# Four transformer layers on one core: reordered loads and stores in the first attention, unit keys' parts moved into its loop, and constant matmuls at each attention's begin

## The chip, the cores and the metric

The kernel is one program on one of the eight cores of a Trainium2 chip. The metric is the device time of one execution in microseconds. A core has five engines with instruction streams of their own: TensorE (PE, matrix products), VectorE (DVE), ScalarE (ACT), GpSimd (POOL) and SyncE (SP, which here only issues transfers). They meet through semaphores. Each engine works strictly through its own list, so an instruction that waits holds back all that stands behind it, transfers that the engine issues included.

## The reference

`x` has 16 batches of 64 tokens with 256 features; `ctx` has the same shape. Four layers follow each other, each of them an attention and a feed-forward:

```python
x = x + L0_xattn(layernorm(x), ctx, ctx)      # 8 heads of 8 features x 256 positions, softmax
x = x + L0_ffn(layernorm(x))                  # ternary weights, quantized activations, two gelus
x = x + L1_xattn(layernorm(x), ctx, ctx)      # as L0, q and k of each head scaled to unit length, x 5
x = x + L1_ffn(layernorm(x))                  # mixture of 8 experts, top 2
x = x + gamma * L2_xattn(layernorm(x), ctx, ctx)   # as L0
x = x + L2_ffn(layernorm(x))                  # mixture of 32 experts, top 8
x = x + L3_xattn(layernorm(x), ctx, mask)     # 16 heads, quantized projections
x = x + L3_ffn(layernorm(x))                  # mixture of 16 experts, top 4
```

In layers 0 to 2 attention takes the 64 x 256 block of one batch as 8 heads of 8 rows: for each head a 256 x 256 matrix of scores, each of them a sum over only 8 features. Scores are wanted at float32 accuracy.

## The kernel before, in words

**Stages.** One function, `attention` (from L417), builds the attentions of layers 0, 1 and 2; `ternary_feed_forward` (from L1614) builds the feed-forward of layer 0; a generic mixture the others. Each is one or more blocks, and at a block's end all engines meet.

**Parts.** A float32 value is split into three bfloat16 values, high, middle and low (`Parts`, L203 on: `high` and `mid` on ScalarE, `take_high` and `take_mid` on GpSimd or VectorE). The parts of normed `x` are stored to DRAM in `q_parts` (`store_q`, L507), those of `ctx` in `k_plain` (`store_k`, L516), and loaded again per batch in another arrangement: `load_q` (L528) writes 288 KB, `load_k` (L538) three times 96 KB. The 72 rows of a head (9 pairs of parts times 8 features) then give a float32 score in one bfloat16 matmul. Tokens are worked in five groups, `CUTS = ((0, 1), (1, 2), (2, 4), (4, 6), (6, 8))`, of tiles of 128 tokens, which are two batches each.

**The loop of an attention with maxima (layers 0 and 2).** For each batch and head TensorE first computes scores into `p_max` (`max_scores`, L669; three buffers), VectorE takes the row maxima (L925), GpSimd splits the 128 x 16 maxima of a batch into three parts (`split_max`, L1019), TensorE turns them (`turn_maxima`, L682), ScalarE copies them (L785) and issues their transfer into rows 72 to 74 of `q` (L790). TensorE then computes the scores again, transposed and with the maximum subtracted (`scores`, L697), ScalarE exponentiates (`exps`, L792), TensorE weighs the values (`weigh`, L715, f32 matmuls), ScalarE copies the result (`copy_out`, L800). Maxima run two batches ahead of the rest (`AHEAD = 16` heads, before the loop). Within a step the order on TensorE is written out by hand, with m for a head's maxima, digits for score pairs, w to z for quarters of the weighing of the batch before, and t for a turn:

```python
FIRST_ORDER = "0mm1mmtmm2mm3mmt"
STEP_ORDER = "mm0mm1wxmmyz2mm3t"
PLAIN_ORDER = "0w1x2yz3"
```

The results go to DRAM (`store_out`, L560) and come back by tile (`load_whole`, L565); VectorE inverts the softmax sums in quarters of a tile between maxima (`invert`, L929, from head n = 61 on, one tile each 16 heads), and GpSimd divides and adds to `x` (`add_tile`, L1034, at even b from 8 on). Layer 1 has no maxima: its queries are normed by `HeadNorm` (L253 on: sums over heads by TensorE, `total_first` and `total_others`; root on ScalarE; inverse on VectorE; spread back by TensorE, `spread_out`).

**SyncE's order in layer 0.** After the first loads: `store_k(0)`, `store_q(0)`, `load_k(0)`, `load_q(0)`, `load_q(1)`, `load_k(1)`, `store_k(1)`, `store_q(1)`, `load_k(2)`, `load_q(2)`, `load_q(3)`, `load_k(3)`, `store_k(2)`, `store_q(2)`. Then, for each step b: `load_k(b + 4)`, `load_q(b + 4)`, `store_out(b - 1)` (which waits for ScalarE's copy of batch b - 1, made in step b), for b = 0 and 1 `store_k(b + 3)` and `store_q(b + 3)`, and from b = 3 on `load_whole(b - 3)`. There are eight slots for `q` and `k`, so a load of batch b + 8 waits until batch b has been scored. ScalarE issues the values' four transfers of 1 MB (`load_v`: one before the loop, the others at the ends of steps 1, 5 and 9).

**Unit keys.** Layer 1's keys are worked out ahead (`UnitKeys`, L318 on). `ctx` in another arrangement (1 MB, `load`) is loaded at the end of step 1; GpSimd adds squares (`add_square`, two feature tiles in each of steps 4 to 7); VectorE clamps the sums behind head 84 (`clamp`). In the feed-forward of layer 0 ScalarE takes the root (`root`, L365), VectorE the reciprocal (`invert`, L369), and GpSimd makes for each of 8 feature tiles the five instructions of `split` (scale, high, rest, middle, low), while SyncE stores each part as it is made (`store_unit_keys`, 24 transfers of 64 KB).

**The feed-forward of layer 0, first block.** VectorE norms `x`, takes row maxima, waits for the mean of the weights (TensorE, from ScalarE's sums over the two raw weights), rounds the first weight in three passes over 128 x 2048 (L1584 to L1586), works out the scale in a dozen short instructions, then rounds each of 8 tiles of `x` in three passes of 128 x 256; TensorE turns a tile (L1707), VectorE copies it (L1785), TensorE multiplies (L1714), ScalarE applies gelu, squares, gelu again. Behind the eighth copy VectorE rounds the second weight and takes maxima of the eight results.

## Time and profile before

| | us |
|---|---|
| median of three runs (1333.0 to 1335.53) | 1334.82 |
| the profiled execution's own time | 1329.65 |
| its span, first to last instruction | 1327.8 |

| stretch of the span | us | TensorE busy | granted clock, mean |
|---|---|---|---|
| attention of layer 0 | 0 to 169.8 | 120.93 | 0.92 |
| feed-forward of layer 0 | 169.8 to 254 | 31.70 | 0.59 |
| attention of layer 1 | 254 to 352 | 79.29 | 0.91 |
| feed-forward of layer 1 | 352 to 501.5 | 130.58 | 0.91 |
| attention of layer 2 | 501.5 to 642 | 111.10 | 0.84 |
| all behind it | 642 to 1327.8 | 612.37 | 0.94 |

TensorE is the busiest engine over the span (82%), before VectorE (51%), ScalarE (48%) and GpSimd (40%). The granted clock is the share of TensorE's full 2.4 GHz that was granted; 0.50 is 1.2 GHz. Two cautions on it: it shows 1.00 before the first change that is on record (71 us), though the matmuls there run at the lower level, so their durations tell the clock better; and a busy share says nothing on whether TensorE was working at 1.2 or at 2.4 GHz.

### The profile page before, as it was taken

Reading aid. Unit: us, or ns where it says so; the run is one execution under the profiler, and the core shown is the slowest. Engines: PE = TensorE matmul, PEld = TensorE weight load, DVE = VectorE, ACT = ScalarE, POOL = GpSimd, SP = SyncE. Lnnn points to the kernel's source line nnn. Section 1 sums busy time; section 2 is a strip of 40 time slices with the busy share of each in tenths; the row PEclk is TensorE's granted clock in tenths of the full one; section 3 lists DMA queues with packets and bytes.
Section 4 is the critical chain, followed back from the end, with each engine's and each line's share of the span. In section 5 each row is a group of like instructions: output and inputs, shape, how many; then the busy total and the mean of one; then the engine's idle time right before and its main releaser. Section 6 shows DMA issues by size and latency. Waiting matters only on the chain. (4 is left out here: it accounts for less than half of the span.)

```text
span 1327.8 us, 19221 instructions
## 1 busy us (share of the span) xinstructions
PE 1086.0 (82%) x6655; PEld 778.3 (59%) x6656; DVE 672.9 (51%) x1377; ACT 636.7 (48%) x1007; POOL 535.4 (40%) x592
## 2 busy tenths in 40 slices
PE   2988714489599994999489999999867569999997
PEld 0445401344288871555378888888634357888886
DVE  5667588741453336787643333333568653333333
ACT  4556537579544434677333344444374334344332
POOL 5132243001236652122256666666310316666663
PEclk9989855789879995899689999999988778999999
DMA  5655121168314314342133343333000013333331
GB/s 172 206 153 161 51 83 28 40 144 224 99 57 123 111 43 132 105 135 77 50 99 111 111 164 121 114 118 114 21 8 1 2 56 125 114 118 114 112 115 55
DMA packets 65796, 132.42 MB, mean 100 GB/s; under 512 B 9291, under 2 KB 33035, under 8 KB 65094
## 3 DMA queue, kind: packets, MB, share of 16 engines
q1 hardware_dynamic: 62326, 124.15, 31.5%
q10 hardware_dynamic: 3408, 7.47, 1.7%
q8 instruction: 35, 0.57, 0.2%
q14 instruction: 27, 0.22, 0.1%
HBM read 115.55 MB, written 15.45 MB: 99 GB/s over the span
## 5 line engine op out<-in xcount | busy, mean ns | idle before, releaser
L1404 POOL TENSOR_TENSOR f_hid<-f_gated,f_coef 128x512 f32<-128x512 f32 x152 | 224.0, 1475 | 161.6 <-DVE f_gated L1435 150.2
L1435 DVE TENSOR_TENSOR f_gated<-f_act_g,f_p_u 128x512 f32<-128x512 f32 x152 | 104.5, 688 | 261.9 <-PE f_p_u L1267 258.1
L796 ACT ACTIVATE a_probs<-a_p_sc 128x1024 f32<-128x1024 f32 x192 | 189.1, 1020 | 31.7 <-PE a_p_sc L710 24.1
L1344 ACT ACTIVATE f_hid_hi<-f_hid 128x512 fp32r<-128x512 f32 x152 | 96.1, 632 | 206.4 <-POOL f_hid L1404 206.3
L925 DVE TENSOR_REDUCE a_maxes<-a_p_max 128x2 f32<-128x512 f32 x256 | 160.0, 680 | 55.0 <-PE a_p_max L677 54.7
L1439 DVE TENSOR_TENSOR f_hid_lo<-f_hid,f_hid_hi 128x512 fp32r<-128x512 f32 x152 | 105.6, 695 | 151.3 <-ACT f_hid_hi L1344 150.9
L1339 ACT ACTIVATE f_act_g<-f_p_g 128x512 f32<-128x512 f32 x152 | 90.8, 597 | 160.8 <-PE f_p_g L1267 160.7
L677 PE MATMUL a_p_max<-a_k,a_q 72*128 72x256 bf16 x512 | 98.9, 318 | 50.4 <-DMA a_q<-q_parts 40.4
L710 PE MATMUL a_p_sc<-a_q,a_k 75*128 75x256 bf16 (+1 forms) x768 | 121.0, 287 | 10.5 <-ACT a_probs L796 4.7
L1280 PE MATMUL f_p_y<-f_hid_hi,f_down_hi 128*128 128x512 f32 x304 | 119.5, 393 | 7.0 <-issue 7.0
L1391 POOL TENSOR_TENSOR f_up_lo<-f_w,f_up_hi 128x512 fp32r<-128x512 f32 x76 | 98.0, 1290 | 56.7 <-ACT f_up_hi L1329 56.7
L1280 PE MATMUL f_p_y<-f_hid_lo,f_down_hi 128*128 128x512 f32 x304 | 119.0, 392 | 0.0
L1280 PE MATMUL f_p_y<-f_hid_hi,f_down_lo 128*128 128x512 f32 x304 | 119.0, 391 | 0.0
L730 PE MATMUL a_p_out<-a_probs,all_v 128*32 128x256 f32 x1536 | 111.8, 406 | 1.2 <-ACT a_probs L796 1.2
L710 PEld LDWEIGHTS a_p_sc<-a_q,a_k 75*128 75x128 bf16 (+1 forms) x768 | 70.4, 102 | 58.9 <-issue 22.8
L1391 POOL TENSOR_TENSOR f_down_lo<-f_w,f_down_hi 128x256 fp32r<-128x256 f32 x76 | 70.7, 931 | 76.6 <-ACT f_down_hi L1334 76.6
L677 PEld LDWEIGHTS a_p_max<-a_k,a_q 72*128 72x128 bf16 x512 | 47.0, 108 | 90.3 <-issue 52.1
L1267 PE MATMUL f_p_g<-f_x_hi,f_up_hi 128*128 128x512 f32 x304 | 96.0, 398 | 0.0
L1267 PE MATMUL f_p_g<-f_x_hi,f_up_lo 128*128 128x512 f32 x304 | 95.4, 395 | 0.0
L1267 PE MATMUL f_p_g<-f_x_lo,f_up_hi 128*128 128x512 f32 x304 | 95.4, 395 | 0.0
L1267 PE MATMUL f_p_u<-f_x_hi,f_up_hi 128*128 128x512 f32 x304 | 95.3, 395 | 0.0
L1267 PE MATMUL f_p_u<-f_x_lo,f_up_hi 128*128 128x512 f32 x304 | 94.7, 393 | 0.0
(283 smaller groups left out, 1682.8 us busy)
## 6 DMA issues: line engine op xcount, KB each, us to landing
f_w<-in_w SPq DMA_DIRECT2D x76, 384.0 KB, 3.5
f_coef<-coef SPq DMA_DIRECT2D x51, 512.0 KB, 3.7
a_q<-q_parts SPq DMA_DIRECT2D x48, 288.0 KB
a_k<-k_plain SPq DMA_DIRECT2D x96, 96.0 KB
outs<-a_out SPq DMA_DIRECT2D x48, 128.0 KB, 1.7
a_whole<-outs SPq DMA_DIRECT2D x48, 128.0 KB, 2.6
q_parts<-a_q_part SPq DMA_DIRECT2D x48, 96.0 KB, 3.2
a_k<-k_unit SPq DMA_DIRECT2D x24, 192.0 KB
```

Of the source, the lines that this page charges most:

```text
L677: last = nc.tensor.matmul(p_max[:, n % 3, t * D:(t + 1) * D], q_of(b, h, ROWS)[:, t * P:(t + 1) * P], k_of(b, h, ROWS), start=True, stop=True)
L710: last = nc.tensor.matmul(p_sc[pair % 2][:, h % 2, t * D:(t + 1) * D], k_of(b, h, K_ROWS)[:, t * P:(t + 1) * P], q_of(b, h, K_ROWS), start ...
L730: last = nc.tensor.matmul(p_out[32 * j:32 * j + 32, 0:D], m.v[:, b, at:at + 32], probs[b % 2][:, h, t, :], start=(quarter == 0), stop=(qua ...
L796: nc.scalar.activation(probs[b % 2][:, 2 * pair:2 * pair + 2, :, :].rearrange("p h t d -> p h (t d)"), p_sc[pair % 2][:], ACT.Exp, scale=s ...
L925: nc.vector.tensor_reduce(maxes[b % 3][:, :, h], p_max[:, n % 3, :].rearrange("p (t d) -> p t d", t=NK), axis=AX.X, op=ALU.max, negate=Tru ...
L1267: last = nc.tensor.matmul(p[:], w_[n][:, (2 * k + s) * P:(2 * k + s + 1) * P], x_[:, k, tok], start=(i == 0), stop=(i == len(passes) - 1))
L1280: last = nc.tensor.matmul(p_y[o][c][:], w_[n][:, o * P:(o + 1) * P], h_[n][c][:], start=start and i == 0, stop=stop and i == len(passes) - ...
L1344: nc.scalar.activation(hid_hi[slot(t, 2)][c][:], hid[c][:], ACT.Copy).then_inc(hid_hi_done, 1)
L1391: nc.gpsimd.tensor_tensor(lo[slot(t, 2)][:], w[slot(t, 2)][:, cols], hi[slot(t, 2)][:], ALU.subtract).then_inc(lo_ready, 1)
L1404: nc.gpsimd.tensor_tensor(hid[c][:], gated[c][:], coef[slot(t, 2)][:, c * 512:(c + 1) * 512], ALU.mult).then_inc(hid_done, 1)
L1435: nc.vector.tensor_tensor(gated[c][:], act_g[c][:], p_u[c][:], ALU.mult).then_inc(gated_done, 1)
L1439: nc.vector.tensor_tensor(hid_lo[slot(t, 2)][c][:], hid[c][:], hid_hi[slot(t, 2)][c][:], ALU.subtract).then_inc(hid_lo_done, 1)
```

## The change

SyncE's order in layer 0 puts all stores of parts, and the loads of batches 0 to 7, before the loop; layer 2 likewise. In the loop the loads are now those of batch b + 7, from b = 1 on, and stand between `store_out(b - 1)` and `load_whole(b - 3)`. At the very begin ScalarE waits for the first tile of `ctx` before it issues the large loads. The unit keys are loaded in the prologue, behind the first values. Their squares are added in steps 2 to 5, the clamp is behind head 68, the root at the end of step 6, the inverse behind head 76, and the five-part splits are one feature tile in each of steps 8 to 15, all of it in the attention's loop; the feed-forward only stores them, with no waits. TensorE gets a filler, 128 x 128 by 128 x 256 bfloat16 matmuls of a constant tile into a part of `p_out` that nothing reads before it is written again: in layer 0, 44 of them once the first query parts are ready, in layer 2, 64; in both, two more behind each of the first ten heads of maxima; in layer 1, 20 ahead of `total_others` and 16 behind it.

```diff
@@ SyncE, layer 0, before the loop
                     store_k(1)
+                    store_k(2)
+                    load_k(2)
                     store_q(1, 0)
                     store_q(1, 1)
-                    load_k(2)
+                    load_k(3)
                     load_q(2)
                     load_q(3)
-                    load_k(3)
-                    store_k(2)
+                    store_k(3)
                     store_q(2, 0)
                     store_q(2, 1)
+                    load_k(4)
+                    store_k(4)
+                    load_q(4)
+                    store_q(3, 0)
+                    store_q(3, 1)
+                    load_k(5)
...
@@ SyncE, loop
-                    elif b + 4 < B:
-                        load_k(b + 4)
-                        load_q(b + 4)
                     if b >= 1:
                         store_out(b - 1)
-                    if with_max and b in (0, 1):
-                        if layer == 0:
-                            store_k(b + 3)
-                        store_q(b + 3, 0)
-                        store_q(b + 3, 1)
+                    if with_max and b >= 1 and b + 7 < B:
+                        load_k(b + 7)
+                        load_q(b + 7)
                     if b >= 3:
                         load_whole(b - 3)
@@ TensorE
+                def keep_busy(count):
+
+                    for _ in range(count):
+                        nc.tensor.matmul(p_out[:, 0:D], m.filler[:, 0:P], m.filler[:], start=True, stop=True)
+
+                pe.wait_ge(m.filler_set, 1)
...
                     pe.wait_ge(masks_loaded[1], 16)
+                    keep_busy(20)
                     unit.total_others(pe)
+                    keep_busy(16)
...
                 if with_max:
+                    parts.ready(pe, 2, 0)
+                    keep_busy(44 if layer == 0 else 64)
                     for n in range(AHEAD):
                         max_scores(n)
+                        if n < HEADS + 2:
+                            keep_busy(2)
@@ ScalarE, layer 0, begin
+                    act.wait_ge(keys_loaded[0], 16)
                     act.dma_start(m.x[:, 1:NI, :], a["x"][:, 1:NI, :]).then_inc(m.x_loaded[1], 16)
+                    key_parts.high(0)
                     act.dma_start(keys[:, 1:NI, :], a["ctx"][:, 1:NI, :]).then_inc(keys_loaded[1], 16)
-                    act.wait_ge(keys_loaded[0], 16)
-                    key_parts.high(0)
...
                     load_v(0)
+                    unit_keys.load(act, a)
@@ ScalarE, loop
-                        if layer == 0 and b == 1:
-                            unit_keys.load(act, a)
+                        if layer == 0 and b == 6:
+                            unit_keys.root(act)
@@ VectorE, loop over heads
-                            if n == 10 * HEADS + 4:
+                            if n == 8 * HEADS + 4:
                                 unit_keys.clamp(dve)
+                            if n == 9 * HEADS + 4:
+                                unit_keys.invert(dve)
@@ GpSimd, loop
-                        if layer == 0 and 4 <= b < 8:
-                            for c in range(2 * (b - 4), 2 * (b - 3)):
+                        if layer == 0 and 2 <= b < 6:
+                            for c in range(2 * (b - 2), 2 * (b - 1)):
                                 unit_keys.add_square(pool, c)
+                        if layer == 0 and b >= B - CH:
+                            if b == B - CH:
+                                for g, (lo, hi) in enumerate(CUTS):
+                                    pool.wait_ge(k_stored[g], 16 * (hi - lo))
+                            for what in range(5):
+                                unit_keys.split(pool, one, what, b - (B - CH))
```

## Rows read from the trace of the kernel before

**Rows 1.** Timeline, ScalarE, attention of layer 0: copies of finished batches (start, duration, what)

```profile
54.66 0.39 ACT L804 ACTIVATE a_out<-a_p_out 128x256 f32<-128x256 f32 x1 [3.71 <-PE a_p_out L730]
...
66.97 0.38 ACT L804 ACTIVATE a_out<-a_p_out 128x256 f32<-128x256 f32 x1 [1.35 <-PE a_p_out L730]
...
82.13 0.39 ACT L804 ACTIVATE a_out<-a_p_out 128x256 f32<-128x256 f32 x1 [3.55 <-PE a_p_out L730]
...
123.27 0.38 ACT L804 ACTIVATE a_out<-a_p_out 128x256 f32<-128x256 f32 x1 [1.27 <-PE a_p_out L730]
...
129.79 0.38 ACT L804 ACTIVATE a_out<-a_p_out 128x256 f32<-128x256 f32 x1 [1.55 <-PE a_p_out L730]
...
141.17 0.38 ACT L804 ACTIVATE a_out<-a_p_out 128x256 f32<-128x256 f32 x1 [2.66 <-PE a_p_out L730]
...
161.86 0.39 ACT L804 ACTIVATE a_out<-a_p_out 128x256 f32<-128x256 f32 x1 [1.19 <-PE a_p_out L730]
```

**Rows 2.** Timeline, ScalarE, attention of layer 2: first and last such copy

```profile
543.32 0.38 ACT L804 ACTIVATE a_out<-a_p_out 128x256 f32<-128x256 f32 x1 [3.17 <-PE a_p_out L730]
...
634.32 0.38 ACT L804 ACTIVATE a_out<-a_p_out 128x256 f32<-128x256 f32 x1 [1.19 <-PE a_p_out L730]
```

**Rows 3.** Timeline, 58 to 72 us: the unit keys' load, and TensorE's longest wait

```profile
58.04 0.70 ACTq L340 DMA_DIRECT2D early_ukeys<-in_ctx_heads  x1
...
71.81 1.01 PE L677 MATMUL a_p_max<-a_k,a_q 72*128 72x256 bf16 x4 [4.36 <-issue]
```

**Rows 4.** Timeline, VectorE and TensorE, 106 to 131 us: three waits

```profile
106.11 0.81 DVE L361 TENSOR_SCALAR early_ulength<-early_ulength 128x256 f32<-128x256 f32 x1 [0.32 <-POOL early_ulength L357]
...
110.35 0.28 PE L692 MATMUL a_p_out<-all_ident_bf,a_neg 128*24 128x128 bf16 x2 [0.87 <-POOL a_neg L1032]
...
130.60 0.55 DVE L935 RECIPROCAL a_inv<-a_whole 128x64 f32<-128x64 f32 x1 [2.52 <-DMA a_whole<-outs]
```

**Rows 5.** Timeline, first steps of the attentions of layers 0 and 2: TensorE, and query parts

```profile
37.20 1.03 PE L710 MATMUL a_p_sc<-a_q,a_k 75*128 75x256 bf16 x4 [2.81 <-DMA a_q<-a_neg_t]
...
49.83 1.94 PE L730 MATMUL a_p_out<-a_probs,all_v 128*32 128x256 f32 x16
...
54.52 0.61 PE L710 MATMUL a_p_sc<-a_q,a_k 75*128 75x256 bf16 x4
...
504.78 0.42 DVE L241 TENSOR_TENSOR a_q_part<-all_xn,a_q_part 128x256 bf16<-128x256 f32 x1 [0.48 <-ACT a_q_part L229]
...
515.55 6.16 PE L677 MATMUL a_p_max<-a_k,a_q 72*128 72x256 bf16 x22 [18.07 <-DMA a_q<-q_parts]
...
526.46 1.03 PE L710 MATMUL a_p_sc<-a_q,a_k 75*128 75x256 bf16 x4 [1.25 <-DMA a_q<-a_neg_t]
```

**Rows 6.** Timeline, feed-forward of layer 0: VectorE, and TensorE's first transposition

```profile
179.81 1.75 DVE L369 RECIPROCAL early_uinverse<-early_ulength 128x256 f32<-128x256 f32 x1
...
181.82 1.70 DVE L1584 TENSOR_SCALAR b_tmp<-b_raw,b_sums 128x2048 f32<-128x2048 f32 x1
...
193.82 0.39 PE L1707 MATMUL b_p_t<-all_ident_bf,b_xq 128*128 128x128 bf16 x2 [14.00 <-DVE b_xq L1586]
...
214.25 1.28 DVE L1584 TENSOR_SCALAR b_tmp<-b_raw,b_sums 128x2048 f32<-128x2048 f32 x1
```

**Rows 7.** Timeline, GpSimd: two unit-key tiles' begins; a maximum's split and the tile behind it

```profile
187.85 0.72 POOL L377 TENSOR_TENSOR early_ukeys<-early_ukeys,early_uinverse 128x256 f32<-128x256 f32 x1
...
191.45 0.72 POOL L377 TENSOR_TENSOR early_ukeys<-early_ukeys,early_uinverse 128x256 f32<-128x256 f32 x1
...
132.37 0.22 POOL L1026 TENSOR_TENSOR a_neg<-a_maxes,a_one 128x16 bf16<-128x16 f32 x1 [7.88 <-DVE a_maxes L925]
...
133.44 0.72 POOL L1039 TENSOR_TENSOR a_prod<-a_whole,a_inv 128x256 f32<-128x256 f32 x1
```

**Rows 8.** Timeline, ScalarE at the begin: a change of activation table

```profile
8.22 1.28 ACT L136 ACT_TABLE_LOAD   x1
```

**Rows 9.** Timeline, TensorE, attention of layer 1: the sums over heads

```profile
266.44 4.77 PE L284 MATMUL a_p_max<-a_qn_square,a_gather 128*128 128x256 f32 x14 [7.73 <-DVE a_qn_square L272]
```

35 lines of the change are left out of this document (23 added, 12 removed).

## The prediction, written before the result was known

> **What bounds the kernel now.** The page says that TensorE is busiest. The question for this change is how much of that it spends waiting or at 1.2 GHz, and where. So the stretches come first (front table): the attentions of layers 0 and 2 have the same loop of 16 batches, yet one takes 169.8 us and the other 140.5. Then I time both loops by ScalarE's copies of finished batches, the last thing done for a batch on the way out. In layer 0 the first copy is at 54.66 and the last at 161.86: 107.2 us [rows 1]. In layer 2 they are at 543.32 and 634.32: 91.0 us for the same 15 intervals, 6.07 on average [rows 2]. The reader is to see two long intervals in layer 0: 66.97 to 82.13 (15.16) and 129.79 to 141.17 (11.38), where a loaded one, 123.27 to 129.79, takes 6.52 [rows 1].
>
> The timelines give their causes. The unit keys' 1 MB is issued at 58.04, with values just ahead of it, and TensorE then stands 4.36 us before it gets the next keys and queries for maxima at 71.81 [rows 3]. At 130.60 VectorE has waited 2.52 us for a tile of outputs to come back, with heads of maxima queued behind it [rows 4]. And at 110.35 TensorE has waited 0.87 us for GpSimd, after VectorE's clamp at 106.11 waited for squares that GpSimd was still adding [rows 4]. Behind each wait TensorE also runs at 1.2 GHz for a while: four score matmuls take 1.01 us at 71.81 [rows 3], 0.61 at 54.52 [rows 5]. So a wait of 1 to 4 us costs 2 to 9.
>
> The second place is each attention's begin: in layer 0 the first scores are at 37.20, at 1.03 for four, and the faster level is first seen at 54.52; in layer 2, from 526.46 to the first copy at 543.32, it is the same [rows 2, 5]. The third is the feed-forward of layer 0, where VectorE holds the path: the unit keys' reciprocal of 1.75 us stands in its list, and a pass over 128 x 2048 takes 1.70 us while GpSimd splits keys and 1.28 when it has stopped [rows 6].
>
> **Layer 0, loads and stores ahead.** Queries of batch 6 are now issued before the loop ends its first step, and nothing of 2 MB can push in front: the keys' load is 30 us earlier, and only the values are left at step 1. The wait at 71.81 goes. Loads for batch b + 7 are five steps ahead of their use. From step 9 on no load is left, so the outputs that VectorE wanted at 130.60 come back without a queue before them. Against that, in steps 4 to 8 `load_whole` now stands behind four load issues. It has about one step before VectorE's first quarter; I take no wait, at most one such as at 130.60, 5.3 us with its slow stretch (11.38 - 6.07). What is late next is TensorE's own chain, as in layer 2. So the loop falls from 107.2 to layer 2's 91.0: -16.2.
>
> **Layer 0's head.** ScalarE gets its first tile of `ctx` sooner, and the chain of group 0 with it. But the unit keys' 1 MB now lands in the prologue, on the same issuing queue ahead of the transfer that the first scores wait for (2.81 us before 37.20 [rows 5]), and SyncE stores group 1's queries later than now. Below, the wait of 2.81 goes; above, 1 MB more, bounded by TensorE's longest wait behind the same load, 4.36 [rows 3]. I take 0 for the first scores. From there to the first copy it was 17.46 us (54.66 - 37.20), in layer 2 16.86 (543.32 - 526.46) [rows 1, 2, 5]: -0.6.
>
> **Unit keys in the loop.** Added to 91.0: VectorE's clamp, 0.81 and perhaps its wait of 0.32 [rows 4]; the reciprocal, 1.75 [rows 6]; ScalarE's root between exponentials, which takes two table changes of 1.28 [rows 8]. At nothing if slack hides them (a step without inverses is shorter than 6.52, so there is some), at most their sum, 5.4, plus one slow stretch of 5.3 = 10.7. They stand on different engines in steps 6 and 7 and each has part of a step's slack. I take +4. GpSimd's splits: a tile takes 3.60 us (187.85 to 191.45), a maximum's split 1.07 (132.37 to 133.44), and every second step adds an `add_tile`, two instructions of 0.72 with their gaps, about 1.5 [rows 7]. That is 6.2 in a step of 6.52 [rows 1]: it fits by 0.3, so 0, up to what the third rival says. The last two splits are behind the last maxima; behind them come `add_tile(4)` and `(5)`, which VectorE's last inverses need: 2 x 3.6 + 3 x 1.5 and one more split, 15 us, beside two steps and a tail that last some 20. Nothing.
>
> **The feed-forward of layer 0.** The reciprocal goes from VectorE's list: -1.75, less perhaps 0.2 as the mean of the weights is then waited for; I take -1.6 [rows 6]. From the first pass at 181.82 to TensorE's first transposition at 193.82 VectorE works beside GpSimd for 12.0 us. At the ratio of the two passes, 1.28 / 1.70, that becomes 9.0: -3.0. The short instructions there hold waits too, so 1.0 (three passes at 0.42 less, 1.3, rounded down) is the least. The loop of eight tiles behind it was in part paced by the same passes; TensorE and ScalarE hold it near, so -0.9 of at most 3. Sum -5.5, range -2.6 to -8. SyncE's 24 stores now come at once behind the two raw weights in one queue. They cost nothing unless they share with the second weight; then up to 3.
>
> **Layer 1.** 14 f32 matmuls in 4.77 us begin at the lower level [rows 9]. At the upper they would be at most halved, -2.4, but they wait for squares; the 16 fillers behind them fill a wait. -1, between 0 and -2.4.
>
> **Fillers in layers 0 and 2.** No row has this matmul; the nearest are four of 256 columns in 1.03 or in 0.61, so 0.26 or 0.15 each [rows 5]. The 64 take 9.8 to 16.5 us and have from 505.20 (504.78 + 0.42) to 515.55, 10.35 [rows 5]. All slow they would delay the start by 6; the clock should rise on the way: 0, with up to +3 for a late rise. They can gain only if the faster level lasts until the first scores. The maxima of the lead are paced by VectorE and gain nothing. Behind the tenth head the fillers end, and there are a turn, five heads and the wait of 1.25 us before 526.46 [rows 5]; in layer 0 the wait is 2.81. A wait of 0.87 was followed by a slow stretch [rows 4]. Moreover, in layer 0 TensorE multiplied scores almost without a break from 37.20 to 49.83 and stayed slow; it got fast only some 4.7 us after the f32 weighing had begun [rows 5]. So I expect the level to be lost before step 0 and steps 0 and 1 to be as now: 0.
> The Trainium skill (TensorE: Matmul & The Clock Gate, "The HAM clock gate") says that any sustained matmul activity releases the throttle, and that long idle gaps bring it back. By that rule the fillers work and layer 2 gains what rival 1 gives; 12 us of score matmuls that released nothing speak against it.
>
> **Sum.** -16.2 - 0.6 + 4 - 5.5 - 1 + 0 = -19.3. The profiled execution took 1329.65, so 1310.35. The median of the runs lies 5.17 higher (1334.82); the same distance kept, 1315.5.
>
> **Rivals.**
> 1. The fillers hold the faster level into steps 0 and 1. The 16.86 us before layer 2's first copy become a short first step and two thirds of a second, 1.67 x 6.07 = 10.1: -6.8; in layer 0 the same if the start isn't late. 1315.5 - 13.6 = 1302, with layer 2 alone 1309. For it: 64 matmuls without a gap just ahead of the loop. Against it: what stands above.
> 2. The moved work costs what it can: 10.7 instead of 4 in steps 6 and 7, and one wait for returned outputs, 5.3: 1315.5 + 12 = 1327.5. For it: the clamp's wait of today comes back in step 6 with the same distance to the squares. Against it: each has slack.
> 3. Slower: GpSimd becomes the bound in steps 8 to 13. If its instructions in the loop are over 5% longer than beside a busy VectorE in the feed-forward (0.3 of 6.2), each turn of the maxima waits for `split_max`; from about 0.9 us on, 18%, each wait is followed by a slow stretch, 5.3 a step. Six steps: +32, 1347. Against it: VectorE's reduction reads PSUM there, and GpSimd's first instruction of a split is 0.72 in the feed-forward, as `add_tile`'s is in the loop [rows 7].
> 4. The prologue's order starves the first scores by a backlog longer than 4.4 us: with 8 us, 1323.
>
> **How the numbers follow.** Forecast 0.57 (own range 1309 to 1322), rival 1 0.18, rival 2 0.13, rival 4 0.07, rival 3 0.05. I call 0.2%, 2.7 us, the least that can be told here. All but rival 3 are faster by more: 0.93; 0.03 in between, 0.04 slower. The range takes in the upper half of rival 1 and most of rival 2: 1300 to 1327.
>
> **What would show it.** In the trace after: no TensorE wait over 2 us in the loop of layer 0, and first to last copy in 92 to 99 us. A wait before the score matmuls of step 7, with table changes on ScalarE. GpSimd nearly without a pause in steps 8 to 13, and TensorE's turn there not over 0.9 us late. VectorE's 128 x 2048 pass at 1.28 in the feed-forward and the first transposition some 5 us after its begin sooner than 24.0 (193.82 - 169.8). Score matmuls of step 0 in both layers at 1.03 for four; 0.61 there proves rival 1. I am wrong in the main point if the interval with the 15.16 stays above 9, or if steps 8 to 13 average above 7.5.

## The result, and the profile after

The changed kernel takes 1345.46 us (median of five runs, 1341.03 to 1350.37) against 1333.19 for the kernel before (five runs): ratio 1.0083, 95% interval 1.0053 to 1.0113. I had forecast 1315.5 and gave slower a chance of 0.04. The profiled execution took 1350.37, its span is 1348.6 us, 20.8 longer than before.

The page of the kernel after; compared with before, TensorE is busy longer and there is more of it at a lower clock:

```profile
span 1348.6 us, 19593 instructions
...
PE 1124.6 (83%) x6840; PEld 808.3 (60%) x6840; DVE 661.7 (49%) x1377; ACT 639.7 (47%) x1009; POOL 532.9 (40%) x593
...
PEclk9677956899789997988689999999978868999999
```

Each stage begins with VectorE's statistics of `x`; the first such instructions cut both spans at the same places.

| stage | before | after | difference |
|---|---|---|---|
| attention of layer 0, from 0 | 169.8 | 178.6 | +8.7 |
| feed-forward of layer 0 | 84.4 | 76.4 | -8.0 |
| attention of layer 1 | 104.4 | 104.1 | -0.2 |
| feed-forward of layer 1 | 141.9 | 141.7 | -0.2 |
| attention of layer 2 | 141.9 | 157.7 | +15.8 |
| all behind it | 685.5 | 690.1 | +4.7 |

The last row is of stages that the change does not touch. Over the seventeen kernels of this document it lies between 684.5 and 692.3 us, so +4.7 is within what it does by itself.

Layer 2 has no unit keys, so the loss there must come from the loads' order or the fillers. ScalarE's copies of finished batches in layer 2 of the kernel after answer to [rows 2]:

```profile
540.78 0.38 ACT L833 ACTIVATE a_out<-a_p_out 128x256 f32<-128x256 f32 x1 [2.79 <-PE a_p_out L747]
...
565.41 0.38 ACT L833 ACTIVATE a_out<-a_p_out 128x256 f32<-128x256 f32 x1 [1.38 <-PE a_p_out L747]
577.60 0.38 ACT L833 ACTIVATE a_out<-a_p_out 128x256 f32<-128x256 f32 x1 [3.40 <-PE a_p_out L747]
...
650.40 0.38 ACT L833 ACTIVATE a_out<-a_p_out 128x256 f32<-128x256 f32 x1 [1.19 <-PE a_p_out L747]
```

The first comes 40.0 us after the stage's begin (before 42.9), but from first to last it is 109.6 us instead of 91.0. Three intervals are long: 12.2 (565.41 to 577.60), 11.5 and 12.9, in steps 5, 7 and 9, where one is usually 6.2 to 6.5. In each VectorE waits before the first quarter of a tile's reciprocals, and TensorE behind it. Timelines of VectorE and TensorE after:

```profile
566.73 0.55 DVE L965 RECIPROCAL a_inv<-a_whole 128x64 f32<-128x64 f32 x1 [3.07 <-DMA a_whole<-outs]
...
585.07 0.55 DVE L965 RECIPROCAL a_inv<-a_whole 128x64 f32<-128x64 f32 x1 [2.66 <-DMA a_whole<-outs]
...
603.61 0.55 DVE L965 RECIPROCAL a_inv<-a_whole 128x64 f32<-128x64 f32 x1 [3.21 <-DMA a_whole<-outs]
```

```profile
567.89 0.39 PE L694 MATMUL a_p_max<-a_k,a_q 72*128 72x256 bf16 x2 [1.78 <-DVE a_maxes L955]
569.66 0.28 PE L709 MATMUL a_p_out<-all_ident_bf,a_neg 128*24 128x128 bf16 x2 [0.94 <-POOL a_neg L1064]
```

It is the wait of [rows 4] (130.60), three times over. The fourth tile has none: no load stands ahead of its `load_whole`, since the last loads are issued in step 8. Six-microsecond stretches of the kernel after show the clock behind it (length, then busy time of PE, PEld, DVE, ACT, POOL; granted clock, DMA share, GB/s): 1.00, then 0.85 with 3.28 us of work in 6, then 0.58 with TensorE busy throughout.

```profile
560.00:566.00 6.00, 6.00 (x66) 3.36 (x63) 3.66 (x6) 4.42 (x7) 0.39 (x2) 1.00 0.47 146
566.00:572.00 6.00, 3.28 (x21) 2.21 (x21) 4.73 (x9) 2.75 (x4) 0.87 (x4) 0.85 0.48 134
572.00:578.00 6.00, 6.00 (x47) 2.60 (x46) 2.94 (x5) 1.91 (x3) 0.81 (x4) 0.58 0.06 13
```

Why the outputs return late stands in SyncE's queue. First the kernel before, then after, in the same step of layer 2 (issues: start, duration, line):

```profile
562.19 0.32 SPq L562 DMA_DIRECT2D outs<-a_out  x1
562.56 0.57 SPq L571 DMA_DIRECT2D a_whole<-outs  x1
563.17 2.03 SPq L546 DMA_DIRECT2D a_k<-k_plain  x3
565.30 0.77 SPq L534 DMA_DIRECT2D a_q<-q_parts  x1
```

```profile
559.66 0.32 SPq L558 DMA_DIRECT2D outs<-a_out  x1
560.02 2.05 SPq L542 DMA_DIRECT2D a_k<-k_plain  x3
562.17 0.77 SPq L530 DMA_DIRECT2D a_q<-q_parts  x1
562.98 0.56 SPq L567 DMA_DIRECT2D a_whole<-outs  x1
```

`load_whole` was issued 0.37 us behind `store_out`; now it is 3.32 us. In the kernel before, the first reciprocal of that tile stood at 566.12, 3.56 us after the issue, without a wait.

Layer 0's copies [rows 1] now come at 54.82, 61.03, 67.19, 80.57, 87.54, 99.18, 106.99, 117.47, 124.00, 136.76 and so on to 170.55: 115.7 us, with four long intervals. Two hold waits of VectorE for returned outputs, 2.63 us at 88.43 and 2.87 at 125.15. The others:

```profile
73.06 1.03 PE L727 MATMUL a_p_sc<-a_q,a_k 75*128 75x256 bf16 x4 [3.76 <-DMA a_q<-a_neg_t]
```

```profile
102.14 1.28 ACT L362 ACT_TABLE_LOAD   x1
103.44 0.42 ACT L362 ACTIVATE early_ulength<-early_ulength 128x256 f32<-128x256 f32 x1
103.87 1.28 ACT L825 ACT_TABLE_LOAD   x1
```

The first is TensorE, which waits for the maxima's rows, in the interval of 13.4 us (the wait of [rows 3] was for keys and queries; it is gone, and this one stands at nearly its place). The second is ScalarE's root with its two table changes. It lies in the interval of 7.8 us that ends at 106.99, and the long one, 10.5 us, comes behind it: VectorE waits 0.55 us for outputs at 106.73, TensorE 0.94 for the split of the maxima at 109.66, and the granted clock is 0.57 from 112 to 117.

At the begin the first scores now come at 34.48 instead of 37.20 [rows 5], but TensorE then waits 2.78 us, with no releaser shown, before its next maxima, so that the first copy does not move (54.82 against 54.66):

```profile
38.29 1.01 PE L694 MATMUL a_p_max<-a_k,a_q 72*128 72x256 bf16 x4 [2.78 <-issue]
```

### The profile page after: what moved, and what is told of

Read it like the earlier page. It is cut to its first block and busy times, and to the rows that moved or that the text cites. A ratio compares the mean times of both kernels' runs of the same rounds, so it can differ in the third digit from the quotient of the medians.

```text
span 1348.6 us, 19593 instructions
## 1 busy us (share of the span) xinstructions
PE 1124.6 (83%) x6840; PEld 808.3 (60%) x6840; DVE 661.7 (49%) x1377; ACT 639.7 (47%) x1009; POOL 532.9 (40%) x593
## 5 line engine op out<-in xcount | busy, mean ns | idle before, releaser
L1472 DVE TENSOR_TENSOR f_gated<-f_act_g,f_p_u 128x512 f32<-128x512 f32 x152 | 104.4, 688 | 261.3 <-PE f_p_u L1304 255.5
L727 PE MATMUL a_p_sc<-a_q,a_k 75*128 75x256 bf16 (+1 forms) x768 | 126.2, 296 | 12.5 <-DMA a_q<-a_neg_t 5.6
L747 PE MATMUL a_p_out<-a_probs,all_v 128*32 128x256 f32 x1536 | 119.2, 428 | 1.2 <-ACT a_probs L825 1.2
L1428 POOL TENSOR_TENSOR f_down_lo<-f_w,f_down_hi 128x256 fp32r<-128x256 f32 x76 | 70.8, 932 | 76.6 <-ACT f_down_hi L1371 76.6
L1304 PE MATMUL f_p_g<-f_x_hi,f_up_lo 128*128 128x512 f32 x304 | 94.9, 394 | 0.0
L1304 PE MATMUL f_p_u<-f_x_lo,f_up_hi 128*128 128x512 f32 x304 | 94.9, 394 | 0.0
L1304 PE MATMUL f_p_u<-f_x_hi,f_up_lo 128*128 128x512 f32 x304 | 94.6, 393 | 0.0
```

What stands on the lines that cost most here:

```text
L727: last = nc.tensor.matmul(p_sc[pair % 2][:, h % 2, t * D:(t + 1) * D], k_of(b, h, K_ROWS)[:, t * P:(t + 1) * P], q_of(b, h, K_ROWS), start ...
L747: last = nc.tensor.matmul(p_out[32 * j:32 * j + 32, 0:D], m.v[:, b, at:at + 32], probs[b % 2][:, h, t, :], start=(quarter == 0), stop=(qua ...
L1304: last = nc.tensor.matmul(p[:], w_[n][:, (2 * k + s) * P:(2 * k + s + 1) * P], x_[:, k, tok], start=(i == 0), stop=(i == len(passes) - 1))
L1428: nc.gpsimd.tensor_tensor(lo[slot(t, 2)][:], w[slot(t, 2)][:, cols], hi[slot(t, 2)][:], ALU.subtract).then_inc(lo_ready, 1)
L1472: nc.vector.tensor_tensor(gated[c][:], act_g[c][:], p_u[c][:], ALU.mult).then_inc(gated_done, 1)
```

## The experiments

**Theory**: `load_whole` behind the loads of batch b + 7 makes VectorE wait in the steps in which it begins a tile; each wait starves TensorE and costs it the upper clock. **Rivals**: the traffic itself and not the order; the unit keys in the loop; the fillers.

All in one table (us). "Whole first" means `load_whole` ahead of the loads on SyncE. "Loop 0" and "loop 2" are first to last copy in layers 0 and 2; "ff 0" is the feed-forward of layer 0; "lead 2" is from the begin of layer 2's attention to its first copy; "ff 1" is the feed-forward of layer 1, which no kernel changes. Stages are of one profiled execution, medians of 5 to 12 runs; ratios are against the kernel before in the same group of runs (its medians there: 1334.11 for e1 to e4, 1335.08 for e5 to e8, 1329.81 for e9 to e12, 1332.18 for e13 to e15).

| kernel | first copy | loop 0 | ff 0 | ff 1 | lead 2 | loop 2 | median | ratio, 95% interval |
|---|---|---|---|---|---|---|---|---|
| before | 54.7 | 107.2 | 84.4 | 141.9 | 42.9 | 91.0 | 1333.19 | |
| after | 54.8 | 115.7 | 76.4 | 141.7 | 40.0 | 109.6 | 1345.46 | 1.0083 (1.0053 to 1.0113) |
| e1 whole first | 53.5 | 102.0 | 76.8 | 138.3 | 41.7 | 91.0 | 1314.09 | 0.9860 (0.9830 to 0.9890) |
| e2 before, whole behind | 53.2 | 122.8 | 85.5 | 142.1 | 42.5 | 116.2 | 1370.46 | 1.0294 (1.0255 to 1.0333) |
| e3 e1, no fillers | 52.9 | 100.4 | 76.6 | 142.0 | 40.5 | 94.3 | 1319.71 | 0.9896 (0.9872 to 0.9920) |
| e4 e1, unit keys back | 53.4 | 94.9 | 85.7 | 142.2 | 40.1 | 94.3 | 1321.27 | 0.9908 (0.9874 to 0.9942) |
| e5 e1, values at step 3 | 54.3 | 101.3 | 76.4 | 141.8 | 40.7 | 94.3 | 1320.74 | 0.9882 (0.9843 to 0.9921) |
| e6 e5, no fillers | 54.4 | 101.1 | 76.5 | 142.1 | 42.7 | 91.0 | 1323.49 | 0.9914 (0.9885 to 0.9943) |
| e7 after, only q ahead | 54.8 | 99.4 | 75.7 | 141.9 | 42.5 | 93.3 | 1322.32 | 0.9907 (0.9872 to 0.9941) |
| e8 after, only k ahead | 53.6 | 107.3 | 76.4 | 138.2 | 41.6 | 102.3 | 1332.48 | 0.9999 (0.9970 to 1.0029) |
| e9 loads alone | 54.0 | 103.7 | 84.3 | 139.6 | 42.5 | 91.0 | 1329.31 | 0.9990 (0.9963 to 1.0018) |
| e10 e1, values at step 2 | 52.5 | 104.2 | 76.0 | 142.0 | 42.4 | 91.0 | 1316.78 | 0.9903 (0.9865 to 0.9941) |
| e11 e10, unit keys early | 55.6 | 106.0 | 76.9 | 137.7 | 41.8 | 91.0 | 1317.44 | 0.9899 (0.9860 to 0.9938) |
| e12 e11, no fillers | 54.0 | 96.7 | 76.3 | 141.8 | 40.4 | 94.3 | 1314.12 | 0.9888 (0.9853 to 0.9923) |
| e13 e1, values by batch | 55.5 | 99.6 | 76.1 | 138.5 | 41.6 | 91.0 | 1311.14 | 0.9853 (0.9808 to 0.9898) |
| e14 e13, unit keys early | 55.0 | 93.3 | 76.3 | 138.4 | 41.6 | 91.0 | 1313.64 | 0.9864 (0.9828 to 0.9901) |
| e15 e14, no fillers | 55.3 | 95.0 | 75.8 | 142.5 | 42.6 | 91.0 | 1315.97 | 0.9870 (0.9828 to 0.9912) |

### The order on SyncE

**e1, on the kernel after:**

```diff
+                    if b >= 3:
+                        load_whole(b - 3)
                     if with_max and b >= 1 and b + 7 < B:
                         load_k(b + 7)
                         load_q(b + 7)
-                    if b >= 3:
-                        load_whole(b - 3)
```

> The changed kernel with one edit: in SyncE's loop load_whole(b - 3) stands directly behind store_out(b - 1), and load_k(b + 7), load_q(b + 7) behind it. Theory (the returned outputs come late because they are issued and queued behind 576 KB of loads, and each wait of VectorE for them starves TensorE and drops its clock): no wait of VectorE for whole in steps 5, 7 and 9 of layer 2, first to last copy there back from 109.6 to 91 us, in layer 0 from 115.7 to about 105; total 1345.5 - 18.6 - 11 = 1316, 1310 to 1322. Rival (the waits come from the traffic itself or from the other engines, the order on the queue decides nothing): both loops within 4 us of the changed kernel's, total over 1338. Rival (fillers or unit keys in the loop made it slower): layer 2 stays near 109 us, since it has no unit keys and the fillers stay.

Measured: layer 2's loop 91.0, total 1314.09, 31 us under the kernel after. The issue is again 0.36 us behind the store, and VectorE's reciprocal comes 3.56 us after it without a wait (SyncE, then VectorE, kernel e1):

```profile
542.31 0.32 SPq L558 DMA_DIRECT2D outs<-a_out  x1
542.67 0.57 SPq L567 DMA_DIRECT2D a_whole<-outs  x1
```

```profile
546.23 0.54 DVE L965 RECIPROCAL a_inv<-a_whole 128x64 f32<-128x64 f32 x1
```

**e2, on the kernel before**, the same in the other direction:

```diff
-                    elif b + 4 < B:
-                        load_k(b + 4)
-                        load_q(b + 4)
                     if b >= 1:
                         store_out(b - 1)
+                    if with_max and b + 4 < B:
+                        load_k(b + 4)
+                        load_q(b + 4)
```

> The kernel before with one edit: load_k(b + 4) and load_q(b + 4) are moved from ahead of store_out(b - 1) to between it and load_whole(b - 3), in the attentions with maxima. Nothing else of the change. Theory: the same waits for returned outputs appear with this edit alone, at the first quarters of tiles 0 to 3 in layer 2, each 5 to 6 us with the slow stretch behind it: its loop 91 to 109-115, layer 0's 107 to 115-122, total 1333 + 20 to 40 = 1353 to 1373. Rival (order decides nothing): 1333 within 3.

Measured: +36 us, with nothing else of the change in it (layer 2's loop +25.2, layer 0's +15.6). `load_whole` is issued 3.32 us behind the store (577.95 and 581.27), and all four tiles of layer 2 wait, the first so:

```profile
584.99 0.55 DVE L935 RECIPROCAL a_inv<-a_whole 128x64 f32<-128x64 f32 x1 [2.36 <-DMA a_whole<-outs]
```

The order alone makes the loss, and taking it back removes it. The traffic rival has fallen: e1 moves the same bytes.

**e7 and e8, on the kernel after**, put half of the loads ahead, 288 KB each, in one issue or in three:

```diff
                     if with_max and b >= 1 and b + 7 < B:
-                        load_k(b + 7)
                         load_q(b + 7)
                     if b >= 3:
                         load_whole(b - 3)
+                    if with_max and b >= 1 and b + 7 < B:
+                        load_k(b + 7)
```

(e8: the same with `load_k` and `load_q` exchanged.)

> The changed kernel with only load_q(b + 7) ahead of load_whole(b - 3), and load_k(b + 7) behind it. Both orders of this pair put 288 KB ahead of the outputs instead of 576; load_q is one issue of 0.77 us, load_k three of 2.1 us together. In layer 2 of the changed kernel load_whole was issued 2.9 us later than it would be behind store_out alone and VectorE waited 2.66 to 3.21 us. Theory A (the issue time decides): 0.8 us later, VectorE waits under 1 us, layer 2's loop 91 to 95, total 1316 to 1322. Theory B (the bytes in the queue decide): half of the wait, 1.3 to 1.6 us, each still followed by a slow stretch: loop 100 to 106, total 1328 to 1338.

> The changed kernel with only load_k(b + 7) ahead of load_whole(b - 3), and load_q(b + 7) behind it: 288 KB and 2.1 us of issues ahead. Theory A (issue time): VectorE waits 1.8 to 2.4 us, with the slow stretch: layer 2's loop 103 to 107, total 1333 to 1342, clearly slower than with load_q ahead. Theory B (bytes): the same as with load_q ahead, within 4 us.

The first tile's reciprocal of e7 and of e8:

```profile
549.72 0.55 DVE L966 RECIPROCAL a_inv<-a_whole 128x64 f32<-128x64 f32 x1 [0.63 <-DMA a_whole<-outs]
```

```profile
552.85 0.55 DVE L966 RECIPROCAL a_inv<-a_whole 128x64 f32<-128x64 f32 x1 [1.58 <-DMA a_whole<-outs]
```

From `store_out` to `load_whole` it is now 1.25 us (e7) and 2.46 (e8). Beyond the 0.37 of before that is 0.88, 2.09 and, in the kernel after, 2.95 later; VectorE's waits in layer 2 are 0.63 to 0.72, 1.58 to 2.31, and 2.66 to 3.21. The wait follows the delay of the issue nearly one for one, and equal bytes gave waits two to three times apart. Theory A holds. So before the change the outputs of layer 2 came back with some 0.3 us to spare. The cost isn't linear: layer 2's loop is 91.0 without a wait, 93.3 with three of 0.7 (about 0.3 an interval, and 1.5 at the end), 102.3 with 1.6 to 2.3 (intervals 7.6, 10.0, 10.0), 109.6 with 2.7 to 3.2 (5 to 6.4 an interval). Between 1.6 and 2.3 the slow clock comes on top: in e8 the granted clock stays 1.00 behind the wait of 1.58, and is 0.54 from 573 to 576, behind that of 2.31 at 567.77.

### What holds layer 0 back once the order is mended

**e5** issues the second values' 1 MB at the end of step 3, **e10** of step 2 (`if layer == 0 and b in (3, 5, 9)` and `(2, 5, 9)`, where it was `(1, 5, 9)`):

> The kernel with load_whole first, and the second values' 1 MB issued at the end of step 3 and not of step 1. The kernel with load_whole first has one long interval of copies left in layer 0 that is not the unit keys': 11.0 us where others take 6.2, with TensorE waiting 2.15 us at 70.10 for the maxima's rows (a_neg_t into a_q), a transfer that was issued at 61.68 behind the 1 MB, in a stretch of 185 to 276 GB/s. Theory (the backlog of the 1 MB is what is late): this wait goes, interval 11.0 to 6.2, total 1314.1 - 4.8 = 1309. Rival (the backlog is of loads for steps 8 to 10, issued there in one go): the interval stays at 10 to 11, total 1314. Rival (the values are then late for step 5): a new wait there, total 1314 to 1320.

> The kernel with load_whole first, and the second values' 1 MB at the end of step 2. At step 1 it stood ahead of a transfer of maxima's rows issued 4 us behind it (wait 2.15 us, interval 11.0), at step 3 it was itself late by 2.18 us at 78.47 (interval 10.6), 9.1 us from issue to use. At step 2 it is issued at about 63.5, used at 76.3, and the rows issued behind it at 68.6 are used at about 76: room on both sides. Theory: no wait in steps 3 to 5, loop 102.0 to 97.5, total 1314 to 1316 in this pair's chip conditions, 4 to 5 us below the kernel with the values at step 3. Rival (traffic of 220 GB/s or more makes one of them late in any place): 10 to 11 stays in one interval.

All three places leave one interval of 10.6 to 11.5 us. TensorE in e1, e5 and e10:

```profile
70.10 1.03 PE L727 MATMUL a_p_sc<-a_q,a_k 75*128 75x256 bf16 x4 [2.15 <-DMA a_q<-a_neg_t]
```

```profile
78.47 1.93 PE L747 MATMUL a_p_out<-a_probs,all_v 128*32 128x256 f32 x16 [2.18 <-DMA all_v<-in_v]
```

```profile
75.72 1.03 PE L727 MATMUL a_p_sc<-a_q,a_k 75*128 75x256 bf16 x4 [2.66 <-DMA a_q<-a_neg_t]
```

Both of my theories for a place with room were wrong. In e5 the rival of values that are late for step 5 was right, in e10 the rival "in any place".

**e9, on the kernel before**, is SyncE's reordering alone, with `load_whole` first:

```diff
+                    store_k(2)
+                    load_k(2)
...
-                    elif b + 4 < B:
-                        load_k(b + 4)
-                        load_q(b + 4)
...
                     if b >= 3:
                         load_whole(b - 3)
+                    if with_max and b >= 1 and b + 7 < B:
+                        load_k(b + 7)
+                        load_q(b + 7)
```

> The kernel before, with SyncE's reordering alone: the changed kernel's order ahead of the loops and its loads of batch b + 7 in them, but load_whole directly behind store_out. Unit keys stay as before, their 1 MB at the end of step 1 with the second values included; no fillers. My prediction's term for the order in layer 0 was -16.2, with the unit keys' load moved too. Theory (the order ahead brings the gain, and the two 1 MB transfers at step 1 only have the maxima's rows behind them): layer 0's loop 95 to 102, with one long interval left behind the 2 MB, total 1334 - 5 to - 12 = 1322 to 1329; the feed-forward of layer 0 as before, 84 us. Rival (the 2 MB now hold back the maxima's rows for as long as they held back the keys): loop 105 to 110, total 1332 to 1338.

```profile
73.98 1.04 PE L731 MATMUL a_p_sc<-a_q,a_k 75*128 75x256 bf16 x4 [5.60 <-DMA a_q<-a_neg_t]
```

The interval of 15.2 us [rows 1] is still 15.1. The wait for keys is gone, and TensorE stands 5.60 us for 12 KB of maxima's rows, issued at 62.12 behind the 2 MB of 56.74 and 57.55 on ScalarE's queue. The loop is 3.5 us shorter, mostly through the wait for outputs at 130.60, which is gone, and the total does not differ (0.9990). Theory (loop 95 to 102) missed; the loop is 103.7, just under the rival's 105.

**e13, on e1:** values of batches 4 to 15 in transfers of 256 KB.

```diff
-                        if layer == 0 and b in (1, 5, 9):
-                            load_v(b // 4 + 1)
+                        if layer == 0 and 1 <= b < 13:
+                            load_v_of(b + 3)
```

> The kernel with load_whole first; values of batches 4 to 15 not in three transfers of 1 MB but in twelve of 256 KB, at the ends of steps 1 to 12, each for the batch three further on. Theory (a burst of 1 MB holds back the small transfer behind it by up to 5 us): no interval over 8.5 us but the unit keys' two (7.8 and 10.0), layer 0's loop 102 to 97, total 4 to 6 us under the ratio 0.986 to 0.990 of its relatives, about 0.983. Rival (the traffic of steps 1 to 4 as a whole is too much): one interval of 10 to 11 stays, ratio 0.986 to 0.990.

```profile
70.67 0.61 PE L727 MATMUL a_p_sc<-a_q,a_k 75*128 75x256 bf16 x4 [0.78 <-DMA a_q<-a_neg_t]
```

The wait is 0.78, the clock is kept (0.61 for four), the interval of 11.0 is 7.0. That points to the burst and not to the amount, but does not prove it. The same 1 MB at the same place was followed by waits of only 0.54 us in e4 and 0.71 in e7 (intervals 6.7 and 6.9). Of the twelve kernels with the new loads and the values in pieces of 1 MB, nine have an interval of over 10 us with a wait of TensorE for the maxima's rows or the values; of the three with pieces of 256 KB none has. And the total did not follow: I expected a ratio of about 0.983, it is 0.9853 against 0.9860 for e1, no difference beyond the intervals. The Trainium skill (DMA: Bandwidth & Descriptors, "Queues, rings and completion order") says that ScalarE's transfers share one ring on each transfer engine, and that an engine takes them in ring order; that fits a 12 KB transfer that is late by the megabyte ahead of it, at 70.10, 73.06 and 73.98. No run here moved the small transfer to another queue. Order within one ring is at least not the whole of it: in e6 and e11 (below) it is outputs on SyncE's queue for which VectorE waits 2.75 and 3.06 us, behind a megabyte of ScalarE's.

### The unit keys

**e4, on e1,** puts root, inverse and splits back into the feed-forward:

```diff
-                            if n == 9 * HEADS + 4:
-                                unit_keys.invert(dve)
...
-                        if layer == 0 and b == 6:
-                            unit_keys.root(act)
...
-                            for what in range(5):
-                                unit_keys.split(pool, one, what, b - (B - CH))
```

> As the kernel with load_whole first, with the unit keys' root, inverse and splits back in the feed-forward of layer 0 (their load stays in the prologue, the squares stay in steps 2 to 5, the clamp at its place). From the changed kernel: the feed-forward stage became 8.0 us shorter with them in the loop, and the interval with root and inverse, 106.99 to 117.47, is 4 us longer than one without. Expect: feed-forward stage +8, layer 0's loop -4 to -6, total +2 to +4 against the kernel with load_whole first. Rival (GpSimd's splits slow steps 8 to 13 as well): loop -8 to -14, total 0 to -6 against it.

The feed-forward is 8.9 us longer. The loop is 7.1 shorter, but 4.3 of that are the interval of 11.0, which is 6.7 in this execution though nothing ahead of it differs, and against that its last steps are 2 us slower. The interval with root and inverse, 7.8, and the one behind it, 10.0, are 6.5 each: 4.8 us. In e1 root (92.45) and inverse (94.20) both lie in the first of the two. The second holds none of the moved work. About its begin TensorE waits 0.60 us for ScalarE (96.56) and 0.94 for the split of the maxima (99.33), and the granted clock is 0.50 from 101 to 104. The clamp (87.11) lies in an interval of 6.5 and costs nothing. Steps 8 to 13 take 6.5 with and without splits, so GpSimd's splits cost nothing.

**e11, on e10,** does squares, clamp, root and inverse before VectorE's first quarter of a tile; **e14** is the same on e13:

```diff
-                            if n == 8 * HEADS + 4:
+                            if n == 5 * HEADS + 4:
                                 unit_keys.clamp(dve)
-                            if n == 9 * HEADS + 4:
+                            if n == 6 * HEADS + 4:
                                 unit_keys.invert(dve)
...
                     split_max(1)
+                    for n in (2, 3, 4):
+                        if layer == 0:
+                            unit_keys.add_square(pool, 2 * n - 4)
+                            unit_keys.add_square(pool, 2 * n - 3)
+                        if n < 4:
+                            split_max(n)
...
-                        if layer == 0 and b == 6:
+                        if layer == 0 and b == 3:
                             unit_keys.root(act)
```

> As the kernel with the values at step 2, and the unit keys' squares, clamp, root and inverse before VectorE's first quarter of a tile (head 61): two squares behind each of split_max 1, 2 and 3 and two in step 2, clamp behind head 44, root at the end of step 3, inverse behind head 52. With load_whole first these parts cost 4.8 us in steps 6 and 7 (intervals 7.8 and 10.0 where 6.5 is usual), where VectorE has eight maxima of 0.69 and two quarters of 0.54 in a step of 6.5, so that its clamp of 0.30 and inverse of 1.75 come on top. GpSimd waits 8.70 and 8.12 us before split_max 2 and 3. Theory (VectorE is what is full there): intervals 7.8 and 10.0 become 6.5, two earlier ones grow by 0 to 1.5; total 3 to 5 us less. Rival (ScalarE's 3 us with two table changes are what costs): the same 4.8 appear in steps 3 and 4, total unchanged.

> The kernel with values by batch, and the unit keys' squares, clamp, root and inverse ahead of VectorE's first quarter. Theory (VectorE is what is full in steps 6 and 7): intervals of 7.8 and 10.0 become 6.5 and one of 7.8 comes in step 3, loop 97 to 93.5, another 3 us less, ratio about 0.981. Rival (ScalarE's table changes cost the same anywhere): within 1 us of the kernel with values by batch.

In e11 a new interval of 11.7 covers the gain: VectorE waits for outputs, with the third values' 1 MB issued ahead of them at 89.58.

```profile
101.21 0.55 DVE L965 RECIPROCAL a_inv<-a_whole 128x64 f32<-128x64 f32 x1 [3.06 <-DMA a_whole<-outs]
```

Without bursts, in e14, the loop is the shortest of all. Its first and last copy:

```profile
54.99 0.38 ACT L840 ACTIVATE a_out<-a_p_out 128x256 f32<-128x256 f32 x1 [3.30 <-PE a_p_out L747]
...
148.29 0.38 ACT L840 ACTIVATE a_out<-a_p_out 128x256 f32<-128x256 f32 x1 [1.19 <-PE a_p_out L747]
```

93.3 us against 99.6 in e13: 8.5 and 9.9 have become 6.5, and step 3 takes 8.1, in which TensorE waits 1.25 us for ScalarE behind the root (74.67). That VectorE is what is full in steps with quarters fits its load (in layer 2 of e1 it is busy 16.57 us of the 18 from 542.7 to 560.7, two quarters a step), but it is not shown. The price in steps 3 and 4 is not a fixed one: these two intervals are 8.1 and 6.5 in e14, 8.1 and 8.1 in e15 and 7.8 and 9.3 in e12, against 6.2 each in layer 2, without the work, which is 2.3, 3.9 and 4.7 us; in e12 the granted clock is 0.50 from 76 to 80. The last is the 4.8 of steps 6 and 7, as the rival has it, and the first is half of it. How far it comes from VectorE, how far from ScalarE's table changes and how far from whether the clock falls stays open. The totals of e13 and e14 do not differ beyond their intervals; the lowest run of all, 1303.43, is e14's.

### The fillers

**e3, e6, e12 and e15** are e1, e5, e11 and e14 without them (layer 1's two groups go too):

```diff
-                    keep_busy(44 if layer == 0 else 64)
...
-                        if n < HEADS + 2:
-                            keep_busy(2)
```

> As the kernel with load_whole first, and without any filler matmul in layers 0, 1 and 2. My prediction's term for the fillers was 0 in all. Read from the changed kernel: layer 2's first copy came 2.9 us sooner after the attention's begin, layer 0's gained nothing, layer 1 0.2. So without them I expect +3 against the kernel with load_whole first, 1316 to 1322. Rival (the fillers hold the clock back or delay maxima in layer 0): without them layer 0's first maxima and first copy are sooner by 1 to 3 and the total is equal or lower. Rival (the fillers save a first step): +7 to +13.

> The kernel with the second values later, without any filler. The pair before (1314.09 with fillers, 1319.71 without, both with load_whole first) differs by 5.6 us, but in the profiled executions layer 2's first copy came 41.7 us after the begin of its attention with fillers and 40.5 without, and layer 0's was at 53.52 with and 52.86 without: the stages that hold fillers show no gain. Theory (my term of 0 holds, and the 5.6 us are spread of the clock elsewhere): within 3 us of the kernel with fillers. Rival (fillers gain something that one profiled execution hides): again 4 to 7 us slower than with them.

> As the kernel with the unit keys early, without any filler. The pairs before gave 5.6 and 2.8 us in favour of the fillers, with a spread of 5 to 6 us in the runs of each. Theory (the fillers gain about 1 us at the begin of layer 2 and 0 to 1 in layer 1): 1 to 4 us slower. Rival (nothing): within 1. Rival (5 or more): they act on the clock further on.

> As the kernel with values by batch and unit keys early, without fillers. Theory (they do next to nothing): within 2 us. Rival: 4 or more slower, as in the first pair.

The four pairs give 5.6, 2.8, -3.3 and 2.3 us in their favour, where the interval of each ratio is worth 3 to 6 us to either side. Lead 2 has a mean of 41.4 with them (ten executions) and 42.0 without (seven). A gain of 1 or 2 us can be neither shown nor excluded; one of 6.8 per attention is excluded. What they do to the clock in layer 2 of the kernel after:

```profile
505.60:508.00 2.40, 2.32 (x12) 1.68 (x13) 2.37 (x9) 0.00 (x0) 0.00 (x0) 0.50 0.21 45
...
510.00:512.00 2.00, 2.00 (x21) 1.78 (x20) 0.89 (x3) 1.57 (x4) 0.00 (x0) 1.00 0.37 90
...
521.00:526.00 5.00, 2.89 (x22) 1.62 (x22) 4.62 (x9) 2.60 (x4) 3.14 (x7) 0.99 0.75 206
526.00:531.00 5.00, 5.00 (x25) 3.21 (x24) 4.29 (x7) 3.05 (x4) 0.65 (x3) 0.50 0.75 216
531.00:536.80 5.80, 5.37 (x26) 3.15 (x24) 4.47 (x8) 2.50 (x4) 0.87 (x4) 0.50 0.48 141
536.80:541.00 4.20, 4.20 (x41) 1.77 (x41) 1.47 (x3) 1.24 (x2) 0.22 (x1) 0.67 0.76 222
```

They do bring the granted clock from 0.50 (1.2 GHz) to 1.00 (2.4 GHz), and all 64, begun at 505.68, take 8.66 us. The first scores are still fast:

```profile
525.04 0.61 PE L727 MATMUL a_p_sc<-a_q,a_k 75*128 75x256 bf16 x4 [0.77 <-DMA a_q<-a_neg_t]
525.49 0.69 PE L694 MATMUL a_p_max<-a_k,a_q 72*128 72x256 bf16 x4
525.97 1.06 PE L727 MATMUL a_p_sc<-a_q,a_k 75*128 75x256 bf16 x4
```

and within a microsecond four take 1.06 again; in the 5 us before (521 to 526) TensorE was busy for 2.89. It returns only with the f32 weighing at 536.86, as before. Mostly the level does not last even that long. Of the ten kernels with fillers seven begin layer 2's scores at 1.03 to 1.06 (only the kernel after and e4 at 0.61, e5 at 0.80), and all ten begin layer 0's at 1.03 or 1.04. The three have the shortest leads of the ten, 40.0 to 40.7, but e3 and e12 without fillers have 40.5 and 40.4.

## Why the prediction was wrong

The step that failed is this sentence: "It has about one step before VectorE's first quarter; I take no wait, at most one such as at 130.60". I had seen that `load_whole` would stand behind four issues. But I took its slack from the code (a step, 6.5 us) and did not read it in the trace. There it is 3.56 us from the issue to the reciprocal, for a way that takes over 3 us: 0.3 us of room, into which 2.95 us of issues were put. And "at most one" was wrong in number: it happens at each of the first three tiles, in both attentions, five waits over 2.6 us and one of 0.55. The price of one, 5.3 us with its slow stretch, was right (4.9 to 6.4). 5 x 6 = 30 us is about what e1 gives back: 1345.46 - 1314.09 = 31.4. The same happened to layer 2, for which I had no term at all: its reordering stood in the diff and in none of my sums.

With the order mended the sum came out: 1314.09 measured, 1315.5 forecast. Not each term did, though (us, e1's profiled execution against that of before):

| term | forecast | e1 | remark |
|---|---|---|---|
| layer 0's loop, loads | -16.2 | -10.0 | -5.2 in all, 4.8 of it unit keys; a wait behind 1 MB took the place of the one removed |
| head | -0.6 | -1.1 | first copy |
| unit keys in the loop | +4 | +4.8 | VectorE and ScalarE, steps 6 and 7 |
| feed-forward of layer 0 | -5.5 | -7.6 | near the outer bound of -8 |
| layer 1 | -1 | -1.0 | -0.2 in the kernel after |
| fillers in 0 and 2 | 0 | -1.2 | lead 2, within its spread |
| not forecast | | -3.6 | feed-forward of layer 1, see below |
| sum | -19.3 | -19.6 | spans 1327.8 and 1308.2 |

So part of the agreement is luck: 6 us too much was expected of the loads, and 5.7 came unforeseen from the feed-forward of layer 0 and a stage that nothing touches. Luck also that the 1345.46 of the kernel after lies near the 1347 of rival 3: the mechanism is another.

Point by point. That the 15.16 would go because "nothing of 2 MB can push in front" was half right: what stands behind the megabytes on ScalarE's own queue, the maxima's rows, was overlooked (13.4 in the kernel after, 11.0 in e1). The sign that I had set, "wrong in the main point if the interval with the 15.16 stays above 9", says wrong. Even in e1 the loop is 102.0, where I had set 92 to 99. Steps 8 to 13 at 6.5 in e1 were right. Rival 2 was half right: the moved work cost 4.8 and not 10.7, but waits for returned outputs did come. Rival 3 (GpSimd) fell: it still waits for VectorE before each split of the maxima in these steps (0.35 to 2.34 us in e1 from 113.91 on, in steps of 6.5), and a unit-key tile takes 3.6 us there as in the feed-forward [rows 7]. The 0.35 is in the steps with an `add_tile`, for which the prediction had worked out 0.3 of room (kernel e1):

```profile
120.44 0.22 POOL L1058 TENSOR_TENSOR a_neg<-a_maxes,a_one 128x16 bf16<-128x16 f32 x1 [0.35 <-DVE a_maxes L955]
```

Rival 4 fell too: the first scores are sooner, not later. In the feed-forward the pass is 1.28 and the first transposition 19.4 us after the begin instead of 24.0, as foreseen:

```profile
178.56 2.71 DVE L149 BATCH_NORM_STATS2 b_ln_stats<-all_x 128x6 f32<-128x256 f32 x8 [0.53 <-PEq L500]
...
189.54 0.16 DVE L1800 TENSOR_SCALAR b_w_mean<-b_p_mean 128x2 f32<-128x2 f32 x1 [1.04 <-PE b_p_mean L1733]
...
189.94 1.28 DVE L1621 TENSOR_SCALAR b_tmp<-b_raw,b_sums 128x2048 f32<-128x2048 f32 x1
```

```profile
197.96 0.39 PE L1739 MATMUL b_p_t<-all_ident_bf,b_xq 128*128 128x128 bf16 x2 [8.52 <-DVE b_xq L1623]
```

VectorE's new wait for the mean of the weights is 1.04, where I took 0.2, and the rest of the stage gave 3.4 us, not 0.9. "0.61 there proves rival 1" was a bad sign to set: the first scores of layer 2 are at 0.61 in the kernel after, and the 6.8 us did not come. There the level is lost not before step 0, as I had it, but in its first microsecond; in layer 0, and in layer 2 of seven of the ten kernels with fillers, it was lost before, as forecast. The Trainium skill (TensorE: Matmul & The Clock Gate, "The HAM clock gate") says that activity releases the throttle and long idle gaps bring it back. The fillers bear out the first half, but other rows do not: a TensorE busy with scores for 10.4 of 10.8 us (526 to 536.8) stays at 0.50. For the second, rows here have the lower level behind waits of TensorE of only 0.77 to 1.96 us, each near other short ones.

## What to carry to other kernels

Before an issue is put ahead of another on a queue, read the slack of the one behind in the trace, from its issue to the first instruction that used it, and hold against it how long it takes: here 3.56 us against over 3, and a few issues in that gap cost 2% of the kernel. Issue time is a cost of its own: three small transfers delay what stands behind them more than one of the same bytes. Loads for later belong behind the small transfer that somebody waits for now. Cutting a large one into pieces, so that a small one never stands behind a megabyte, shortened the loop here (102.0 to 99.6, one execution each) but not measurably the total.
